# Two graph networks with residual layer norms on one core: the last layer norm's split rows turned by DMA instead of by TensorE

## The chip, the cores and the metric

The kernel runs on one core of a Trainium2 chip. The metric is the device time of one execution in microseconds (us), as the median of several runs. The profile is of one further execution, whose engines are named PE (TensorE; PEld are its weight loads), DVE (VectorE), ACT (ScalarE), POOL (GpSimd) and SP (SyncE, which here only issues DMAs).

## What is computed

The input `x` is 128 graphs x 128 nodes x 128 features. Two networks follow each other, each with a residual and a layer norm over the features:

```
x1  = layernorm(x  + gnn0(x,  adj))          # graph mix, two dense layers, batch norms
out = layernorm(x1 + gnn1(x1, adj))          # two graph layers, then the LSTM part

# LSTM part of gnn1, on h of shape (128 graphs, 128 nodes t, 128 features)
for p in 1, 2, 3, 4:
    nw   = 128 // p
    wins = h[:, :nw*p, :] as windows of p consecutive nodes
    last = last hidden state of LSTM_p over each window
    h[:, p-1::p, :] = last                   # the last node of each window is replaced
```

After the four periods, node `t` of `h` holds the state that period 4 wrote if `t % 4 == 3`; the other three of each four nodes hold what the periods 1 to 3 left there.

## The kernel before, in words

**The early part** (to about 350 us) computes `x1`, spills it to a scratch tensor in HBM, runs the two graph layers and, between them, the LSTM steps of period 1. The change does not touch its work. Two constants of it, `minus_c` and `u1_bias`, lie in SBUF and are last read there.

**The late part** is a list of LSTM steps, the units, written `p.tile.s` (period, tile of 4 windows x 128 graphs = 512 columns, step in the window). `LATE` gives the order of units 32 to 128 by hand. A first step (`s = 0`) has three gates of three 128x512 matmuls, 9 in all; a later step has four gates of six, 24 in all, since inputs and states are fp16 pairs of a high and a low half. For one unit, PE sums the gates into a ring of six PSUM banks (`lstm_unit`), ACT applies the gate functions (L894) and the tanh of the cell (L901), and DVE does `cell` (L1096, or L1099, L1101 and L1103), `hidden` (L1110), and splits the result into `hist`: `hidden_hi` (a cast, L1115) and `hidden_lo` (L1120). The last step of period 4 is `kept`: its result stays fp32 in `acts` and is not split.

**The last layer norm** is spread over the late part. Nodes are taken in 8 tiles of 16; a piece is one tile and one residue `r` of the node number modulo 4, so 4 nodes x 128 graphs. `hist` has the features on the partitions and the norm wants them on the free axis, so each piece is turned. For `r = 0, 1, 2` PE multiplies the high and the low half with an fp16 identity and sums them in PSUM: 8 matmuls (L798, L799, in `turn_h`). For `r = 3` PE transposes the four fp32 blocks of `acts` (L796). DVE adds the PSUM bank to the rows of `x1`, which a 1 MB load has brought into one of six SBUF buffers (`end_add`, L1175), then takes four row statistics (`end_row_stats`, L1182); after `r = 2` and after `r = 3` five small operations give the moments (`end_moments`, L1133 to L1140). POOL takes the power -1/2 (L534) and scales the rows (L544), and SP writes them out (L473). Once both parts of tile 0 (tile 1) are written, the buffer takes `x1` of tile 6 (7).

**The order** around the change is set by `ln_slots`, which places each piece at a unit number: PE turns it behind that unit, DVE adds it in the next unit between `cell` and `hidden`. SP follows the order of the moments. All engines wait only on semaphores in these fixed orders.

Of the kernel before, what the change touches and what calls it, by code (L numbers as in the profile page):

```python
# [8 lines left out]
ALU = mybir.AluOpType  # L9
# [142 lines left out]
def ln_slots():  # L152


    turns, adds, moments = {}, {}, {}
# [20 lines left out]
    for at, piece in sorted(places):  # L176
        put(turns, at, piece)
        put(adds, at + 1, piece)
        if piece[1] >= 2:
            put(moments, at + 1, (piece[0], 0 if piece[1] == 2 else 3))  # L180
    return turns, adds, moments


TURNS, ADDS, MOMENTS = ln_slots()


# [4 lines left out]
TURN_ORDER, ADD_ORDER, MOMENT_ORDER = (in_order(t) for t in (TURNS, ADDS, MOMENTS))  # L191
# [3 lines left out]
assert TURN_ORDER == ADD_ORDER  # L195
# [7 lines left out]
def resnorm_gnn_kernel(nc, x, adj, W1, b1, g1, be1, W2, b2, g2, be2,  # L203
# [15 lines left out]
    with ExitStack() as ctx:  # L219
# [24 lines left out]
        minus_c = sb("minus_c", [P, CB, P])  # L244
        u1_bias = sb("u1_bias", [P, CB, P])
# [99 lines left out]
        x1_loaded = [sem(f"x1_loaded{k}") for k in range(X1_RING)]  # L345
        h_turned, end_added, end_stats_done, end_step, end_var, end_rstd, end_scaled, tail_scaled = (
# [47 lines left out]
        def unit_cell(n):  # L394
            u = UNITS[n]
            if u.p == 1:
                return acts[:, n % 2, G, :]
            return cell_bufs[u.p, u.tile % CELLS[u.p]][:, 0:u.cols]

# [4 lines left out]
        def _(sp):  # L404
# [62 lines left out]
            for n, piece in enumerate(MOMENT_ORDER):  # L467
# [10 lines left out]
                if piece[1] == 3 and tile + X1_RING < TILES:  # L478
                    sp.wait_ge(out_written[tile % X1_RING], 32 * (tile // X1_RING + 1))
                    load_x1(tile + X1_RING)  # L480
            for k in range(X1_RING):
# [4 lines left out]
        def _(pool):  # L486
# [42 lines left out]
            for n, piece in enumerate(MOMENT_ORDER):  # L529
# [6 lines left out]
                if n >= N_POOLED:  # L536
                    continue
# [8 lines left out]
                last.then_inc(end_scaled, 1)  # L546

        @block.tensor
        def _(pe):
# [233 lines left out]
            def turn_h(tile, r):  # L783

                n = TURN_ORDER.index((tile, r))
                last = NUMBER[Unit(4, tile, 3)]
                if r == 3:
                    pe.wait_ge(hid_done, last + 1)
                else:
                    pe.wait_ge(lo_done, halves_through(max(NUMBER[v] for v in sources(Unit(4, tile, 0)))))  # L790
                wait(pe, end_added, n - 1)
                for m in range(CB):
                    t = tile * T_TILE + 4 * m + r
                    acc = ps[:, TURN + n % 2, m * P:(m + 1) * P]
                    if r == 3:
                        done = nc.tensor.transpose(acc, acts[:, last % 2, O, m * P:(m + 1) * P], ident[:])  # L796
                        continue
                    nc.tensor.matmul(acc, hist[:, 0, t, :], ident16[:], start=True, stop=False)  # L798
                    done = nc.tensor.matmul(acc, hist[:, 1, t, :], ident16[:], start=False, stop=True)  # L799
# [26 lines left out]
            for n in range(N_EARLY, len(UNITS)):  # L826
                lstm_unit(n)
                for tile, r in TURNS.get(n, ()):
                    turn_h(tile, r)
# [134 lines left out]
        def _(dve):  # L964
# [188 lines left out]
            def relu_h0(g, h):  # L1153
                dve.wait_ge(h0_summed, 2 * g + h + 1)
                nc.vector.tensor_tensor(h0T[:, h * CB:(h + 1) * CB, :].rearrange("p b n -> p (b n)"), ps[:, H0[h], :],  # L1155
                                        minus_c[:].rearrange("p b n -> p (b n)"), ALU.max).then_inc(h0_copied, 1)

            def bias_u1(g, h):
                dve.wait_ge(u1_summed, 2 * g + h + 1)
                nc.vector.tensor_tensor(u1[:, h * CB:(h + 1) * CB, :].rearrange("p b n -> p (b n)"), ps[:, U1[h], :],  # L1160
                                        u1_bias[:].rearrange("p b n -> p (b n)"), ALU.add).then_inc(u1_copied, 1)
# [8 lines left out]
            def end_add(tile, r):  # L1170
                n = ADD_ORDER.index((tile, r))
                rows = x1_tile[tile % X1_RING].rearrange("p (m r) d -> p r m d", r=4)[:, r, :, :]
# [4 lines left out]

            def end_row_stats(tile, r):
                rows = x1_tile[tile % X1_RING].rearrange("p (m r) d -> p r m d", r=4)[:, r, :, :]
                dve.wait_ge(end_added, ADD_ORDER.index((tile, r)) + 1)  # L1180
# [3 lines left out]
            def end_moments(piece):  # L1184
                n = MOMENT_ORDER.index(piece)
                tile, rows = piece[0], moment_rows(piece)
                dve.wait_ge(end_stats_done, CB * (ADD_ORDER.index((tile, rows.stop - 1)) + 1))
# [118 lines left out]
```

## Time and profile before

| | us |
|---|---|
| median of 3 runs (lowest, highest) | 757.35 (756.95, 757.46) |
| the profiled execution, its own time | 757.01 |
| its span (first to last instruction) | 755.2 |
| PE busy | 737.3 |
| DVE busy | 657.6 |
| ACT busy | 538.8 |
| POOL busy | 316.5 |

The time of the profiled execution is 1.8 us more than its span, and 0.34 us below the median. A row of the timeline gives start, duration, engine, line, operation, and in brackets the idle time just before it. Matmuls are pipelined: a row says 0.38 us for a 128x512 matmul, while the next one starts 0.22 us after it. DVE operations overlap a little too; what one costs is read from start to start. A row of a stretch gives its bounds and length, then the busy time (and instructions) of PE, PEld, DVE, ACT and POOL, the granted TensorE clock as a share of full speed, the DMA share and GB/s.

### The profile page before, as it was taken

The page shows a single profiled execution, that of the slowest core. Times are in us where ns is not written, and L with a number is a line of the kernel's source. Part 1 is how long each engine was busy: PE and PEld are TensorE (multiplying, and loading weights), DVE is VectorE, ACT ScalarE, POOL GpSimd, SP SyncE. Part 2 cuts the span into 40 slices and gives each one's busy share as a digit, 9 for nine tenths or more (in the row PEclk, how much of TensorE's full clock was granted, in tenths as well). Part 3 has the DMA queues.
Part 4 walks back from the last instruction along what each step waited for, and adds up shares of the span by engine and source line. Part 5 has one row for each costly group of instructions (what it writes and reads, how often), then busy time and mean ns, then how long its engine had stood idle before and what let it go on. Part 6 is the DMA issues. An engine that isn't in the chain of part 4 may idle for free.

```text
span 755.2 us, 11504 instructions
## 1 busy us (share of the span) xinstructions
PE 737.3 (98%) x4016; PEld 426.6 (56%) x4016; DVE 657.6 (87%) x1391; ACT 538.8 (71%) x872; POOL 316.5 (42%) x287
## 2 busy tenths in 40 slices
PE   8999999999999999998999999999999999999994
PEld 6777644677777777673444444444444444554542
DVE  6888787888998989858998799889999898899987
ACT  4877898467777686659887686786676767666662
POOL 1000000159788887800000001600981946239986
PEclk9999999999999999999999999999999999999997
DMA  5642400024424334114300000100000121021012
GB/s 158 189 140 87 112 1 1 1 56 112 112 57 113 83 86 111 30 29 193 141 1 2 0 1 1 43 1 0 28 35 24 38 75 43 1 70 57 15 56 85
DMA packets 64606, 45.08 MB, mean 60 GB/s; under 512 B 1658, under 2 KB 63524, under 8 KB 63524
## 3 DMA queue, kind: packets, MB, share of 16 engines
q1 hardware_dynamic: 64548, 44.33, 19.2%
q8 instruction: 33, 0.54, 0.3%
q14 instruction: 25, 0.20, 0.1%
HBM read 27.55 MB, written 16.78 MB: 59 GB/s over the span
## 4 chain that ended last, share of the span: by engine, by line
PE 53%; DVE 15%; ACT 6%; issue 2%; POOL 1%; DMA 1%; POOLq 0%; DVEq 0%; SPq 0%
PE ps L660 10%; PE ps L661 10%; PE ps L669 10%; PE ps L674 7%; PE ps L665 7%; PE ps L666 7%; ACT work L894 4%; DVE ln_stats L1146 2%; DVE ring L1127 2%; DVE store L1166 2%; DVE ring L1155 2%; DVE work L1110 1%; ACT work L901 1%; DVE work L1096 1%; DVE ring L1160 1%
## 5 line engine op out<-in xcount | busy, mean ns | idle before, releaser
L894 ACT ACTIVATE work<-ps,gate_bias 128x512 f32<-128x512 f32 x449 | 282.6, 680 | 91.1 <-PE ps L674 57.9
L660 PE MATMUL ps<-store,wih 128*128 128x512 f16 (+1 forms) x443 | 166.7, 376 | 2.3 <-ACT work L894 2.3
L661 PE MATMUL ps<-store,wih 128*128 128x512 f16 (+1 forms) x443 | 166.7, 376 | 0.0
L669 PE MATMUL ps<-store,wih 128*128 128x512 f16 (+1 forms) x443 | 156.0, 376 | 0.0
L534 POOL TENSOR_TENSOR end_mv<-end_mv,minus_half 128x12 f32<-128x12 f32 (+1 forms) x16 | 31.0, 1940 | 256.0 <-DVE end_mv L1140 256.0
L525 POOL TENSOR_SCALAR ring<-ring,ln_mv 128x128 f32<-128x128 f32 x112 | 113.3, 1024 | 2.8 <-POOL ln_mv L513 2.7
L1110 DVE TENSOR_TENSOR work<-work 128x512 f32<-128x512 f32 (+1 forms) x129 | 88.2, 684 | 22.5 <-ACT work L901 22.5
L901 ACT ACTIVATE work<-store 128x512 f32<-128x512 f32 x97 | 60.5, 623 | 52.7 <-DVE store L1103 36.2
L665 PE MATMUL ps<-store,whh 128*128 128x512 f16 (+1 forms) x248 | 93.2, 376 | 0.0
L666 PE MATMUL ps<-store,whh 128*128 128x512 f16 (+1 forms) x248 | 93.1, 376 | 0.0
L674 PE MATMUL ps<-store,whh 128*128 128x512 f16 (+1 forms) x248 | 93.0, 376 | 0.0
L544 POOL TENSOR_SCALAR ring<-ring,end_mv 128x128 f32<-128x128 f32 x72 | 85.7, 1202 | 1.4 <-POOL end_mv L534 1.4
L1120 DVE TENSOR_TENSOR store<-work,store 128x512 f16<-128x512 f32 (+1 forms) x121 | 81.9, 676 | 1.4 <-ACT store L926 1.4
L660 PEld LDWEIGHTS ps<-store,wih 128*128 128x128 f16 x443 | 43.4, 98 | 53.1 <-issue 8.2
L669 PEld LDWEIGHTS ps<-store,wih 128*128 128x128 f16 x443 | 43.3, 98 | 50.9 <-DVE store L1120 0.3
L661 PEld LDWEIGHTS ps<-store,wih 128*128 128x128 f16 x443 | 43.3, 98 | 48.3 <-issue 5.0
L505 POOL TENSOR_SCALAR bn_rstd<-mean_var 128x1 f32<-128x1 f32 x3 | 0.6, 193 | 134.0 <-DVE mean_var L1062 76.2
L544 POOL TENSOR_SCALAR store<-store,end_mv 128x128 f32<-128x128 f32 x48 | 54.9, 1156 | 1.1 <-POOL end_mv L534 1.1
L845 ACT ACTIVATE store<-ps,vec 128x512 f32<-128x512 f32 x64 | 40.5, 684 | 13.5 <-PE ps L589 13.4
L1099 DVE TENSOR_TENSOR work<-work 128x512 f32<-128x512 f32 (+1 forms) x62 | 42.3, 682 | 8.5 <-ACT work L894 7.5
L1031 DVE BATCH_NORM_STATS2 st<-store 128x6 f32<-128x512 f32 x64 | 41.2, 685 | 8.7 <-ACT store L845 8.6
L1101 DVE TENSOR_TENSOR store<-work,store 128x512 f32<-128x512 f32 (+1 forms) x62 | 42.1, 680 | 7.5 <-ACT work L894 7.4
(135 smaller groups left out, 1285.8 us busy)
## 6 DMA issues: line engine op xcount, KB each, us to landing
ring<-in_x_dram SPq DMA_DIRECT2D x32, 256.0 KB, 2.9
ring<-in_x_dram SPq DMA_DIRECT2D x16, 512.0 KB, 5.3
x_scratch<-ring SPq DMA_DIRECT2D x16, 512.0 KB, 3.5
ring<-x_scratch SPq DMA_DIRECT2D x5, 1024.0 KB, 4.9
out_dram<-ring SPq DMA_DIRECT2D x5, 768.0 KB, 3.5
store<-x_scratch SPq DMA_DIRECT2D x3, 1024.0 KB, 14.0
out_dram<-store SPq DMA_DIRECT2D x3, 768.0 KB, 3.9
out_dram<-ring SPq DMA_DIRECT2D x5, 256.0 KB, 2.3
```

Source lines behind the costliest of these rows:

```text
L525: last = nc.gpsimd.tensor_scalar(row, row, mv[:, 1, b:b + 1], mv[:, 4, b:b + 1], ALU.subtract, ALU.mult)
L544: last = nc.gpsimd.tensor_scalar(row, row, mv[:, 1, k:k + 1], mv[:, 4, k:k + 1], ALU.subtract, ALU.mult)
L660: nc.tensor.matmul(acc(j), w_hi, x_hi, start=True, stop=False)
L661: nc.tensor.matmul(acc(j), w_lo, x_hi, start=False, stop=False)
L665: nc.tensor.matmul(acc(j), w_hi, h_hi, start=False, stop=False)
L666: nc.tensor.matmul(acc(j), w_lo, h_hi, start=False, stop=False)
L669: last = nc.tensor.matmul(acc(j), weights(wih, j)[0], x_lo, start=False, stop=u.first)
L674: nc.tensor.matmul(acc(j), weights(whh, j, 1)[0], h_lo, start=False, stop=True)\
L894: nc.scalar.activation(acts[:, n % 2, gate, 0:u.cols], ps[:, gate_bank(q), 0:u.cols], ACT.Tanh if gate == G else ACT.Sigmoid, bias=gate_bi ...
L901: nc.scalar.activation(tanh_c[:, n % 2, 0:UNITS[n].cols], unit_cell(n), ACT.Tanh)\
L1110: nc.vector.tensor_tensor(hid, hid, tanh_c[:, n % 2, 0:u.cols], ALU.mult).then_inc(hid_done, 1)
L1120: nc.vector.tensor_tensor(unit_output(u, 1), columns(acts[:, n % 2, O, :], u), unit_output(u, 0), ALU.subtract).then_inc(lo_done, 1)
```

## The change

- PE no longer turns the pieces with `r < 3`; `turn_h` keeps `r = 3` alone.
- SP turns them instead (`move_rows`). Per tile it issues 8 transposing DMAs from `hist` to a new buffer `h_rows`: for each half (high, low) and each group of 4 nodes, 128 x 384 fp16 values become 3 blocks of 128 x 128. That is 96 KB each and 768 KB a tile, 64 DMAs in all.
- `h_rows` holds one tile. It lies over `minus_c` and `u1_bias`, and the first DMA of a tile waits until DVE has added the whole tile before (`h_added`).
- DVE adds a piece in two steps, high rows and then low rows, both from SBUF (`add_halves`); the second waits for the first, and each waits for its half's DMAs (`h_moved`).
- `ln_slots` places the pieces anew: a tile is moved one unit after its last source has run, and its first piece is added at the earliest four units after that. So the pieces of a tile come earlier than before in some places, and in the order of tiles 0 to 7.
- On SP the moves and the output writes are interleaved by unit number, a write standing four units behind its moments (`OUT_DELAY`).

```diff
     for tile in range(P // T_TILE):
-        ready = max(NUMBER[v] for v in sources(Unit(4, tile, 0))) + 2
-        wanted.append((max(ready, NUMBER[Unit(4, tile, 0)]), tile))
+        written = max(NUMBER[v] for v in sources(Unit(4, tile, 0)))
+        put(moves, written + 1, tile)
+        wanted.append((written + 4, tile))
...
+            def move_rows(tile):
+                n = MOVE_ORDER.index(tile)
+                sp.wait_ge(lo_done, halves_through(max(NUMBER[v] for v in sources(Unit(4, tile, 0)))))
+                wait(sp, h_added, 6 * n)
+                for s in range(2):
+                    for m in range(CB):
+                        t = tile * T_TILE + 4 * m
+                        sp.dma_start(h_rows[:, s, 3 * m:3 * m + 3, :],
+                                     hist[:, s, t:t + 3, :].rearrange("p t b -> p (t b)"),
+                                     transpose=True).then_inc(h_moved[s], 16)
...
-                    t = tile * T_TILE + 4 * m + r
-                    acc = ps[:, TURN + n % 2, m * P:(m + 1) * P]
-                    if r == 3:
-                        done = nc.tensor.transpose(acc, acts[:, last % 2, O, m * P:(m + 1) * P], ident[:])
-                        continue
-                    nc.tensor.matmul(acc, hist[:, 0, t, :], ident16[:], start=True, stop=False)
-                    done = nc.tensor.matmul(acc, hist[:, 1, t, :], ident16[:], start=False, stop=True)
+                    done = nc.tensor.transpose(ps[:, TURN + n % 2, m * P:(m + 1) * P],
+                                               acts[:, last % 2, O, m * P:(m + 1) * P], ident[:])
...
+            def add_halves(tile, r):
+                n = MOVE_ORDER.index(tile)
+                rows = x1_tile[tile % X1_RING].rearrange("p (m r) d -> p r m d", r=4)[:, r, :, :]
+                dve.wait_ge(x1_loaded[tile % X1_RING], 16 * (tile // X1_RING + 1))
+                for s in range(2):
+                    dve.wait_ge(h_moved[s], 16 * CB * (n + 1))
+                    wait(dve, h_added, 6 * n + 2 * r + s)
+                    nc.vector.tensor_tensor(rows, h_rows[:, s, :, :].rearrange("p (m r) d -> p r m d", r=3)[:, r, :, :],
+                                            rows, ALU.add).then_inc(h_added, 1)
```

Which pieces stand in which unit, by `ln_slots` (unit numbers; `(tile, r)`):

| tile | added before, r = 0, 1, 2 | moved now | added now, r = 0, 1, 2 |
|---|---|---|---|
| 0 | 62, 63, 64 | 59 | 63, 64, 65 |
| 1 | 81, 82, 83 | 69 | 73, 74, 75 |
| 2 | 77, 78, 79 | 72 | 76, 77, 78 |
| 3 | 90, 91, 92 | 82 | 86, 87, 88 |
| 4 | 98, 99, 100 | 92 | 96, 98, 99 |
| 5 | 111, 112, 113 | 94 | 100, 101, 102 |
| 6 | 117, 118, 119 | 113 | 117, 118, 119 |
| 7 | 121, 122, 124 | 116 | 120, 121, 122 |

The order of DVE's instructions in units 74 to 77 (3.5.0, 3.7.0, 4.2.0, 3.5.1), before, from `hidden` of unit 74 on. L1110 is `hidden`, L1115 and L1120 the two halves, L1096 the `cell` of a first step.

```order
671 L1110 TENSOR_TENSOR work<-work 128x512
672 L1115 CAST store<-work 128x512
673 L1096 TENSOR_TENSOR store<-work 128x512
674 L1120 TENSOR_TENSOR store<-work,store 128x512
675 L1110 TENSOR_TENSOR work<-work 128x512
676 L1115 CAST store<-work 128x512
677 L1096 TENSOR_TENSOR store<-work 128x512
678 L1120 TENSOR_TENSOR store<-work,store 128x512
679 L1110 TENSOR_TENSOR work<-work 128x512
```

The same stretch now, where the lines of these operations are L1135, L1140, L1145 and L1121, with the piece (1, 2), its moments and the piece (2, 0):

```order
677 L1121 TENSOR_TENSOR store<-work 128x512
678 L1145 TENSOR_TENSOR store<-work,store 128x512
679 L1210 TENSOR_TENSOR ring<-turned,ring 128x4x128 x2
680 L1220 BN_STATS end_stats<-ring 128x6 x4
681 L1158 TENSOR_TENSOR end_mv<-end_stats 128x12
...
685 L1165 SCALAR_TENSOR_TENSOR end_mv<-end_mv 128x12
686 L1135 TENSOR_TENSOR work<-work 128x512
687 L1140 CAST store<-work 128x512
688 L1121 TENSOR_TENSOR store<-work 128x512
689 L1145 TENSOR_TENSOR store<-work,store 128x512
690 L1210 TENSOR_TENSOR ring<-turned,ring 128x4x128 x2
691 L1220 BN_STATS end_stats<-ring 128x6 x4
```

Each `x2` is the high and the low add of one piece. Between the last add of tile 1 (row 679) and the first of tile 2 (row 690) stand the statistics, the moments, `hidden`, the cast, `cell` and the low half.

On SP, where the rows before held output writes and two loads alone, this stands now from the first move on:

```order
60 L485 DMA_TRANSPOSE turned<-store 128x3x128 x16
61 L496 DMA out_dram<-ring 128x4x384
62 L485 DMA_TRANSPOSE turned<-store 128x3x128 x8
63 L496 DMA out_dram<-ring 128x4x384
64 L485 DMA_TRANSPOSE turned<-store 128x3x128 x8
65 L496 DMA out_dram<-ring 128x4x384
66 L485 DMA_TRANSPOSE turned<-store 128x3x128 x8
```

Eight transposing DMAs a tile; the moves of tiles 0 and 1 follow each other directly, and each later one stands behind the write of an earlier tile.

## Rows read from the trace of the kernel before

**Rows 1.** The page's first part: busy time and share of the span, whole run.

```profile
PE 737.3 (98%) x4016; PEld 426.6 (56%) x4016; DVE 657.6 (87%) x1391; ACT 538.8 (71%) x872; POOL 316.5 (42%) x287
```

**Rows 2.** Chain of waits, 352 to 745 us: shares by line; then start us, us, what.

```profile
by line: PE ps L660 18.4%; PE ps L661 18.3%; PE ps L669 18.3%; PE ps L674 13.1%; PE ps L665 13.1%; PE ps L666 13.1%; PE ps L799 1.4%; PE ps L798 1.4%; PE ps L796 0.7%; ACT work L894 0.4%; DVE store L1101 0.3%; issue 0.3%; DVE end_stats L118
...
352.02 0.70 ACT work L894
...
737.18 0.70 ACT work L894
```

**Rows 3.** Who waited for whom, 352 to 743 us: engine line, releaser, us, times, longest.

```profile
ACT work L894 <- PE ps L674: 57.3, 110, 1.1
...
PE ps L660 <- ACT work L894: 0.5, 1, 0.5
```

**Rows 4.** Busy time of the engines in four stretches of the late stage.

```profile
443.70:505.30 61.60, 61.60 (x304) 28.59 (x303) 55.70 (x102) 46.20 (x73) 16.72 (x13) 1.00 0.04 14
505.30:590.30 85.00, 85.00 (x449) 40.74 (x448) 79.58 (x167) 59.09 (x95) 43.12 (x31) 1.00 0.06 20
590.30:651.80 61.50, 61.50 (x325) 30.73 (x324) 53.10 (x107) 42.22 (x70) 33.70 (x27) 1.00 0.14 48
651.80:743.50 91.70, 91.70 (x500) 46.02 (x499) 84.73 (x210) 57.53 (x92) 71.93 (x60) 1.00 0.13 42
```

**Rows 5.** PE in order of time, the turn after unit 3.6.1: start us, us, engine, line.

```profile
564.10 0.22 PE L798 MATMUL ps<-ident,store 128*128 128x128 f16 x1
...
564.54 0.38 PE L660 MATMUL ps<-store,wih 128*128 128x512 f16 x1
```

**Rows 6.** The turn's matmuls by line, whole run: duration ns min/median/max.

```profile
L798 PE MATMUL ps<-ident,store x96: 219/219/219, 447.4 to 717.0; 128*128 128x128 f16 x96
```

**Rows 7.** DVE in order of time, hidden(n) of units 82 to 86.

```profile
540.73 0.67 DVE L1110 TENSOR_TENSOR work<-work 128x512 f32<-128x512 f32 x1
...
545.36 0.69 DVE L1110 TENSOR_TENSOR work<-work 128x512 f32<-128x512 f32 x1
...
547.87 0.69 DVE L1110 TENSOR_TENSOR work<-work 128x512 f32<-128x512 f32 x1 [0.17 <-ACT work L901]
...
551.93 0.69 DVE L1110 TENSOR_TENSOR work<-work 128x512 f32<-128x512 f32 x1 [0.17 <-ACT work L901]
...
556.00 0.69 DVE L1110 TENSOR_TENSOR work<-work 128x512 f32<-128x512 f32 x1 [0.16 <-ACT work L901]
```

**Rows 8.** DVE in order of time, one whole unit (3.8.1) with a piece.

```profile
602.03 0.69 DVE L1110 TENSOR_TENSOR work<-work 128x512 f32<-128x512 f32 x1
...
605.77 0.68 DVE L1175 TENSOR_TENSOR store<-ps,store 128x512 f32<-128x512 f32 x1
606.49 0.87 DVE L1182 BATCH_NORM_STATS2 end_stats<-store 128x6 f32<-128x128 f32 x4
607.28 0.67 DVE L1110 TENSOR_TENSOR work<-work 128x512 f32<-128x512 f32 x1
```

**Rows 9.** DVE in order of time, first and last hidden of the 70 units summed.

```profile
443.72 0.69 DVE L1110 TENSOR_TENSOR work<-work 128x512 f32<-128x512 f32 x1 [0.16 <-ACT work L901]
...
745.77 0.69 DVE L1110 TENSOR_TENSOR work<-work 128x512 f32<-128x512 f32 x1 [0.16 <-ACT work L901]
```

**Rows 10.** DMA: the queue (packets, MB, share); issues with us to landing; SP's issues.

```profile
q1 hardware_dynamic: 64548, 44.33, 19.2%
...
store<-x_scratch SPq DMA_DIRECT2D x3, 1024.0 KB, 14.0
...
out_dram<-ring SPq DMA_DIRECT2D x5, 256.0 KB, 2.3
...
348.57 1.28 SPq L458 DMA_DIRECT2D ring<-x_scratch  x3
```

**Rows 11.** Busy time and granted clock after the last gate (same columns as rows 4).

```profile
743.50:746.50 3.00, 0.56 (x5) 0.32 (x3) 2.80 (x6) 1.32 (x2) 2.82 (x4) 1.00 0.64 227
746.50:748.00 1.50, 0.66 (x4) 0.42 (x4) 1.43 (x10) 0.00 (x0) 1.25 (x3) 0.79 0.00 0
```

More of the change, by code:

```diff
@@ L152, in ln_slots @@
 def ln_slots():
-    turns, adds, moments = {}, {}, {}
+    moves, turns, stats, moments = {}, {}, {}, {}
     end = len(UNITS) - 1
@@ L176, in ln_slots @@
     for at, piece in sorted(places):
-        put(turns, at, piece)
-        put(adds, at + 1, piece)
+        if piece[1] == 3:
+            put(turns, at, piece)
+        put(stats, at + 1, piece)
         if piece[1] >= 2:
             put(moments, at + 1, (piece[0], 0 if piece[1] == 2 else 3))
-    return turns, adds, moments
-TURNS, ADDS, MOMENTS = ln_slots()
+    return moves, turns, stats, moments
+MOVES, TURNS, STATS, MOMENTS = ln_slots()
 def in_order(table):
     return [piece for n in sorted(table) for piece in table[n]]
-TURN_ORDER, ADD_ORDER, MOMENT_ORDER = (in_order(t) for t in (TURNS, ADDS, MOMENTS))
+MOVE_ORDER, TURN_ORDER, STAT_ORDER, MOMENT_ORDER = (in_order(t) for t in (MOVES, TURNS, STATS, MOMENTS))
+assert MOVE_ORDER == [tile for tile, r in STAT_ORDER if r == 0]
+OUT_DELAY = 4
 TAIL = MOMENTS[len(UNITS) - 1]
@@ L480, in _ @@
                     load_x1(tile + X1_RING)
+            for n in range(N_EARLY, len(UNITS) + OUT_DELAY):
+                for tile in MOVES.get(n, ()):
+                    move_rows(tile)
+                for piece in MOMENTS.get(n - OUT_DELAY, ()):
+                    write_rows(piece)
             for k in range(X1_RING):
@@ L527, in _, with scale_rows @@
                 last.then_inc(x1_ready, 1)
[L529 removed]
+            def scale_rows(piece):
+                n = MOMENT_ORDER.index(piece)
                 tile, rows = piece[0], moment_rows(piece)
@@ L546, in _ @@
                 last.then_inc(end_scaled, 1)
+            for n in range(N_EARLY, len(UNITS)):
+                for piece in MOMENTS.get(n, ()):
+                    scale_rows(piece)
         @block.tensor
@@ L827, in _ @@
                 lstm_unit(n)
-                for tile, r in TURNS.get(n, ()):
-                    turn_h(tile, r)
+                for tile, _ in TURNS.get(n, ()):
+                    turn_h(tile)
         @block.scalar
@@ L1246, in _ @@
                 if n < end:
-                    for tile, r in ADDS.get(n, ()):
-                        end_add(tile, r)
+                    for tile, r in STATS.get(n, ()):
+                        if r == 3:
+                            end_add(tile)
+                        else:
+                            add_halves(tile, r)
                         end_row_stats(tile, r)
@@ L1252, in _ @@
                 else:
-                    for tile, r in ADDS[end][:-1]:
-                        end_add(tile, r)
+                    for tile, _ in STATS[end][:-1]:
+                        end_add(tile)
                 hidden(n)
@@ L1257, in _ @@
                     hidden_hi(n)
-            for tile, r in ADDS[end]:
-                if (tile, r) == ADDS[end][-1]:
-                    end_add(tile, r)
+            for tile, r in STATS[end]:
+                if (tile, r) == STATS[end][-1]:
+                    end_add(tile)
                 end_row_stats(tile, r)
```

41 lines of the change are left out of this document (23 added, 18 removed).

## The prediction, made before the changed kernel was run

> **What bounds the kernel now.** Read the page's first part first: PE is busy for 737.3 us, 98% of the span, and DVE comes next with 87% [rows 1]. Then the chain of waits. From 352.02 us, where ACT ends the graph part, to 737.18 us every share above 0.7% is a line of PE, and the turns of the split rows, L798 and L799, hold 1.4% each [rows 2]. The waits say the same from the other side: ACT waited 57.3 us for sums of PE, and PE waited 0.5 us, once [rows 3]. So in the late stage PE is the bound, and the turns lie on the path.
>
> The stretches then show how near the next bound is. In the four of rows 4, 299.8 us together, PE has no gap, and DVE is busy for 55.70 + 79.58 + 53.10 + 84.73 = 273.1 us, which leaves 26.7 us idle [rows 4]. Not all of that is spare. A unit on a loaded DVE still shows a wait of 0.17 us before `hidden`, for the tanh of ACT [rows 7]. Over the 69 units of these stretches that is 11.7 us that no added work can take, since added work only moves it. **The real spare is about 15 us in 300.** An independent count agrees. Between `hidden` of unit 58 and of unit 128 lie 302.1 us [rows 9]; 21 first steps at 2.51 us and 49 later ones at 4.07 us [rows 7], with the pieces below, come to between 285 and 290 us.
>
> **What the change removes from PE.** Each of the 24 pieces costs PE eight small matmuls. One says 0.22 us [rows 6], but they overlap: from the start of the first to the start of the next unit's first matmul it is 564.54 - 564.10 = 0.44 us [rows 5]. 24 x 0.44 = 10.6 us leave PE. If PE stayed the bound, the profiled execution's 757.0 us would become 746.4 us.
>
> **What it adds to DVE.** Before, a piece is one add of 128x512 from PSUM and four statistics. The add starts at 605.77 and the statistics, which wait for it, at 606.49, so a dependent add costs 0.72 us; the statistics take 0.79 us more [rows 8]. Now there are two adds, the second dependent on the first. The operand from SBUF instead of PSUM should change nothing: `hidden`, with both operands in SBUF, takes 0.69 us against 0.68 us for the add [rows 7, 8]. The trace has no add that mixes fp16 and fp32 inputs alone, so between 0 and 0.72 us I take the upper end, as the same form and size. 24 x 0.72 = 17.3 us, on an engine with 15 us to spare: 2.3 us over the present end, and the 10.6 us of PE are gone with it. DVE becomes the bound.
>
> **The new places make it uneven.** A piece adds 5.25 - 4.07 = 1.2 us net to a later unit now [rows 7, 8], 1.9 us after the change. The moments add 0.7 us. Tiles 1 and 2 are now added back to back in units 73 to 78, of which 74, 75 and 76 are first steps, where PE needs 9 x 0.216 = 1.9 us and DVE 2.51 us without any piece. For units 73 to 79 PE needs 4 x 5.2 + 3 x 1.9 = 26.5 us, DVE 4 x 4.07 + 3 x 2.51 + 6 x 1.9 + 2 x 0.7 = 36.6 us. PE can run ahead of ACT by its six banks only, 1.5 later units or 7.8 us, so this burst alone stops PE for 2 us or more, depending on how far DVE lags when it begins. Units 96 to 102 carry seven pieces in the same way. Between the bursts, in units 66 to 72, 103 to 108 and 124 to 126, there is no split piece and DVE will catch up and idle, so part of the 15 us is out of reach. I take 4.5 us, three tenths of it, as an estimate (0 to 8).
>
> **The transposing DMAs.** SP has no work of its own, and their issue costs nobody else anything. What counts is the time L from the release of a tile's eight DMAs to the landing of the last. No row shows such a DMA. From below: three plain issues took 1.28 us, 0.43 us each, and an output of 256 KB landed 2.3 us after issue [rows 10]: 7 x 0.43 + 2.3 = 5.3 us. From above: three loads of 1 MB queued behind others took 14.0 us to land [rows 10], for a tile's 768 KB. In between, by packets: the queue moved 64548 in 19.2% of 16 x 755.2 us, 36 ns each on its engine [rows 10]. Cut into rows of 128 fp16 values, a tile has 3072 packets, 192 on each engine, 6.9 us; with 2.3 us to land L is 9.2 us. I take this, since it counts the pieces that a turned block must be written in. The Trainium skill ("Advanced Engine Details and Errata", X-Bar Transpose (TRN2)) says instead that transposing DMAs are as fast as plain ones, 350 to 400 GB/s; by that the data take some 2 us and the sum would come to rival 2, about 765 us. No row here shows which.
>
> Where is L hidden? For tiles 0, 1, 3, 4 and 6 the first add stands five units behind the last source: some 11 to 15 us by 5.2 and 1.9 us a unit. At 9.2 us they are covered. **Tiles 2, 5 and 7 are not.** The buffer holds one tile, so their DMAs start only with the last add of tile 1, 4 or 6, in units 75, 99 and 119, and the first add that needs them is in the very next unit. Between the two DVE has the statistics, the moments, `hidden`, the cast, `cell` and the low half. For a first step this is 545.36 - 540.73 - 0.72 = 3.9 us [rows 7], for the later step 5.25 - 0.72 + 0.7 = 5.2 us. The low rows are needed 0.7 us later. Cover in all: 3.9 + 5.2 + 3.9 + 3 x 0.7 = 15.1 us against 3 x 9.2 = 27.6 us. DVE stands still for 12.5 us, with `hidden`, hence the split halves that PE waits for, queued behind. As DVE is the bound by then, all of it counts. On SP the output writes queue behind these waiting moves; POOL's scaling is finished late anyway and the end does not move.
>
> **Sum**, against the profiled execution: 757.0 + 2.3 + 4.5 + 12.5 = 776.3 us. That execution lies 0.34 us under the median of the runs, within their spread, so I predict 776.
>
> **Rivals.**
> 1. *Faster: DVE takes it.* If the second add costs less than (15 - 4.5) / 24 = 0.44 us and L stays under some 5 us, DVE still fits below the old end, and PE's saving shows, down to 746.4 us if all of it does. For it: PE is the only bound today. Against it: every two-input operation of this size on DVE has 0.67 to 0.69 us [rows 7, 8], and even L's lower bound is 5.3 us. Chance 0.15.
> 2. *Slower, but only by DVE's work.* L is near 5.3 us: 757.0 + 2.3 + 4.5 + (15.9 - 15.1) = 764.6 us. Chance 0.17, and 0.03 that pieces and stage gains cancel to no change.
> 3. *Much slower: the DMAs run one behind the other.* If each transposing DMA takes its own 2.3 us to land before the next moves, L is 8 x 2.3 = 18.4 us. Then the three bare hand-overs cost 55.2 - 15.1 = 40.1 us and the five others about 5 x (18.4 - 14.5) = 19.5 us: 757.0 + 6.8 + 59.6 = 823 us. It decides from L above some 14 us. For it: the trace has no transposing DMA that would exclude it. Chance 0.20. The Trainium skill ("VectorE: DVE Perf Modes", The three transpose paths) gives 1309 ns for one 128x128 block by DMA; 24 blocks in a row would be 31 us, further on this side than any row.
>
> A smaller cost sits in all of them: after PE had been nearly idle for 3 us, the granted clock of the next stretch was 0.79 [rows 11]. Stops of PE at the three hand-overs could cost about 1 us each this way; it is in the range, not in the sum.
>
> **How the numbers follow.** The forecast (L between 6 and 14 us, 767 to 794 us) has 0.45. The range of 752 to 825 us takes in rivals 2 and 3 and the milder part of rival 1, and leaves out the full gain and an L above 18 us. Faster by over 0.2% (what a measurement of this kernel can tell from no change) 0.15, within 0.2% 0.03, slower 0.82.
>
> **What would show it.** In the profile after: no L798 or L799 rows; DVE at over 90% of the span; PE with idle time in the late stage whose releaser is DVE's cast or low half, none of which it has now; DVE's high-rows add waiting for a DMA at three places, first after unit 75, by some 4 us each; landing of the transposing DMAs of 9 us a tile; the dependent adds 0.72 us apart. It would be wrong if PE still showed no gap, if the adds took clearly under 0.7 us, or if tiles 0, 1, 3, 4 and 6 waited too.

## The result, and the profile after

The changed kernel takes **798.54 us** (median of 4 runs, 797.52 to 798.67), the kernel before 757.40 us beside it (4 runs, 756.95 to 757.57). The ratio is 1.054, with a 95% interval of 1.0527 to 1.0553: slower by 41 us, where 18.6 us were forecast. 798.5 us lies inside the predicted range, and above the 767 to 794 us that the forecast's own case allowed. Two runs in a slow state are left out of every number below: one of experiment 5 (1093.89 us, at a granted clock of 0.654) and one of the kernel before (780.88 us, at 0.946).

The first part of the page of the kernel after, which answers to [rows 1], its row of PE in tenths, the queue that moves the tiles (packets, MB, share of the 16 DMA engines), and the chain by engine; the last row is the chain of the kernel before:

```profile
span 796.7 us, 11215 instructions
PE 737.4 (93%) x3824; PEld 415.8 (52%) x3824; DVE 674.2 (85%) x1415; ACT 535.3 (67%) x872; POOL 305.7 (38%) x287
PE   8999999999999999989999999858999958999394
q1 hardware_dynamic: 91172, 50.63, 22.3%
DVE 35%; PE 23%; ACT 10%; issue 5%; SPq 4%; DMA 2%; POOL 1%; DVEq 0%; POOLq 0%
PE 53%; DVE 15%; ACT 6%; issue 2%; POOL 1%; DMA 1%; POOLq 0%; DVEq 0%; SPq 0%
```

DVE was busy for 674.2 - 657.6 = 16.6 us more, the 24 added adds at 0.69 us each. PE, with 192 matmuls fewer, now has gaps (the 5, 5 and 3 in its row of tenths). DVE leads the chain now, and SP's queue and the DMAs are in it; before, PE led it, and in the late part it was nearly PE alone [rows 2].

The same four stretches as [rows 4], by time from the span's start (they hold fewer units now):

```profile
443.70:505.30 61.60, 59.67 (x276) 26.49 (x274) 56.37 (x104) 44.76 (x72) 16.76 (x13) 1.00 0.17 39
505.30:590.30 85.00, 71.55 (x319) 31.07 (x317) 73.60 (x156) 47.34 (x78) 37.10 (x30) 0.94 0.15 38
590.30:651.80 61.50, 55.04 (x250) 24.44 (x248) 53.01 (x110) 34.59 (x57) 32.89 (x28) 0.94 0.27 73
651.80:743.50 91.70, 79.78 (x391) 38.21 (x388) 72.10 (x162) 53.42 (x90) 44.48 (x40) 0.96 0.17 45
```

PE is idle for 13.5 of the 85.0 us of the second stretch, and DVE for 11.4, against 5.4 us before: DVE is not busier than it was, it stands still. The waits from 350 us on say for what (engine, line, releaser, us, times, longest; L926 is ACT's tanh of the cell, L1210 the new adds, L694 the first matmul of a gate, L823 the turn of `r = 3`):

```profile
ACT work L926 <- DVE store L1128: 94.1, 62, 10.6
PE ps L694 <- ACT work L919: 24.8, 10, 8.2
PE ps L823 <- DVE work L1135: 15.2, 2, 13.0
DVE ring L1210 <- DMA turned<-store: 8.7, 2, 4.4
DVE ring L1210 <- issue: 6.4, 2, 3.2
DVE store L1210 <- DMA turned<-store: 4.4, 1, 4.4
DVE store L1210 <- issue: 1.2, 1, 1.2
```

The last four are the waits of the first adds of tiles 2, 5 and 7 and of no others, 7.6, 5.6 and 7.5 us: 8.7 + 6.4 + 4.4 + 1.2 = **20.7 us**. PE, which waited for ACT for 0.5 us before [rows 3], now waits for ACT and for `hidden` (once for 13.0 us, behind the wait of tile 7), and those wait for DVE.

One hand-over in full. DVE in order of time (start, us, engine, line, operation, idle before) from the last add of tile 1 to the first of tile 2, in unit 76:

```profile
513.28 1.48 DVE L1210 TENSOR_TENSOR ring<-turned,ring 128x512 f32<-128x512 f16 x2
514.79 0.87 DVE L1220 BATCH_NORM_STATS2 end_stats<-ring 128x6 f32<-128x128 f32 x4
...
516.30 0.69 DVE L1135 TENSOR_TENSOR work<-work 128x512 f32<-128x512 f32 x1
...
517.96 0.68 DVE L1145 TENSOR_TENSOR store<-work,store 128x512 f16<-128x512 f32 x1
521.89 0.72 DVE L1210 TENSOR_TENSOR ring<-turned,ring 128x512 f32<-128x512 f16 x1 [3.25 <-issue]
526.99 0.69 DVE L1210 TENSOR_TENSOR ring<-turned,ring 128x512 f32<-128x512 f16 x1 [4.37 <-DMA turned<-store]
```

And the chain of waits over the same time (start, us, what), followed back from the end:

```profile
514.07 0.70 DVE ring L1210
514.83 1.19 SPq L485
516.06 1.26 SPq L485
517.36 1.26 SPq L485
518.66 1.26 SPq L485
519.96 1.26 SPq L485
521.25 1.98 SPq L485
523.27 1.26 SPq L485
524.58 2.39 DMA turned<-store
526.99 0.70 DVE ring L1210
```

The last add of tile 1 frees the buffer at 514.8. SP then needs about 1.26 us for **each issue** (each SPq row is one; the sixth took 1.98 us). The eighth starts at 524.58, and 2.4 us after this start its data are there: L = 526.99 - 514.83 = 12.2 us. For tiles 5 and 7 L was 11.4 and 12.1 us (the first issue at 629.04 and 730.08, the low add at 640.47 and 742.19). The four stretches of 10 us around the first hand-over, PE alone (busy, granted clock, DMA share, GB/s):

```profile
505.00:515.00 10.00, 6.97 (x32) 1.00 0.00 0
515.00:525.00 10.00, 9.91 (x46) 1.00 0.35 71
525.00:535.00 10.00, 1.85 (x5) 0.61 0.27 89
535.00:545.00 10.00, 8.84 (x36) 0.88 0.00 1
```

DVE stops at 518.6 us. PE works on with its six banks until 524.9 us, 6.3 us longer, where 7.8 us of run ahead were forecast, and then has nothing for 8.2 us. With the stop the mean granted clock of the stretch falls to 0.61, between its levels of 1.2 and 2.4 GHz. The transposing DMAs by themselves, whole run:

```profile
L485 SPq DMA_TRANSPOSE turned<-store x64: 1182/1257/2306, 446.6 to 739.8; - x64
DMA to landing us min/median/max: 2.3/2.4/4.1
```

The queue took (22.3% x 796.7 - 19.2% x 755.2) x 16 = 523 us of packet time for 91172 - 64548 = 26624 packets more than before [rows 10]. Put down to the 64 DMAs alone, as an estimate, that is 20 ns a packet and 523 / 64 / 16 = 0.5 us a DMA on each engine, against 1.26 us for its issue: the DMA engines were not the limit.

### The profile page after: what moved, and what is told of

Read it like the earlier page. It is cut to its first block, busy times and chain, and to the rows that moved or that the text cites. A ratio compares the mean times of both kernels' runs of the same rounds, so it can differ in the third digit from the quotient of the medians.

```text
span 796.7 us, 11215 instructions
## 1 busy us (share of the span) xinstructions
PE 737.4 (93%) x3824; PEld 415.8 (52%) x3824; DVE 674.2 (85%) x1415; ACT 535.3 (67%) x872; POOL 305.7 (38%) x287
## 3 DMA queue, kind: packets, MB, share of 16 engines
q1 hardware_dynamic: 91172, 50.63, 22.3%
## 4 chain that ended last, share of the span: by engine, by line
DVE 35%; PE 23%; ACT 10%; issue 5%; SPq 4%; DMA 2%; POOL 1%; DVEq 0%; POOLq 0%
ACT work L919 6%; DVE work L1135 4%; PE ps L694 4%; PE ps L695 4%; PE ps L703 4%; SPq L485 3%; ACT work L926 3%; PE ps L708 3%; PE ps L699 3%; PE ps L700 3%; DVE store L1126 3%; DVE store L1145 3%; DVE work L1124 2%; DVE ln_stats L1171 2%; DVE end_stats L1220 2%
## 5 line engine op out<-in xcount | busy, mean ns | idle before, releaser
L919 ACT ACTIVATE work<-ps,gate_bias 128x512 f32<-128x512 f32 x449 | 279.1, 680 | 72.4 <-PE ps L708 39.2
L694 PE MATMUL ps<-store,wih 128*128 128x512 f16 (+1 forms) x443 | 168.8, 381 | 26.2 <-ACT work L919 26.1
L695 PE MATMUL ps<-store,wih 128*128 128x512 f16 (+1 forms) x443 | 168.7, 381 | 0.0
L703 PE MATMUL ps<-store,wih 128*128 128x512 f16 (+1 forms) x443 | 157.3, 379 | 0.0
L926 ACT ACTIVATE work<-store 128x512 f32<-128x512 f32 x97 | 60.5, 623 | 115.7 <-DVE store L1128 94.1
L1135 DVE TENSOR_TENSOR work<-work 128x512 f32<-128x512 f32 (+1 forms) x129 | 89.0, 690 | 22.0 <-ACT work L926 22.0
L699 PE MATMUL ps<-store,whh 128*128 128x512 f16 (+1 forms) x248 | 95.0, 383 | 2.2 <-DVE store L1140 2.2
L708 PE MATMUL ps<-store,whh 128*128 128x512 f16 (+1 forms) x248 | 94.1, 380 | 1.6 <-DVE store L1145 1.6
L700 PE MATMUL ps<-store,whh 128*128 128x512 f16 (+1 forms) x248 | 94.9, 383 | 0.0
L694 PEld LDWEIGHTS ps<-store,wih 128*128 128x128 f16 x443 | 43.6, 98 | 85.2 <-ACT work L919 24.4
L1145 DVE TENSOR_TENSOR store<-work,store 128x512 f16<-128x512 f32 (+1 forms) x121 | 81.9, 677 | 1.4 <-ACT store L951 1.4
L574 POOL TENSOR_SCALAR ring<-ring,end_mv 128x128 f32<-128x128 f32 x72 | 78.2, 1098 | 1.4 <-POOL end_mv L564 1.4
L574 POOL TENSOR_SCALAR store<-store,end_mv 128x128 f32<-128x128 f32 x48 | 52.0, 1095 | 1.1 <-POOL end_mv L564 1.1
L1124 DVE TENSOR_TENSOR work<-work 128x512 f32<-128x512 f32 (+1 forms) x62 | 42.4, 684 | 11.7 <-ACT work L919 10.3
L870 ACT ACTIVATE store<-ps,vec 128x512 f32<-128x512 f32 x64 | 40.5, 683 | 13.5 <-PE ps L623 13.5
L1056 DVE BATCH_NORM_STATS2 st<-store 128x6 f32<-128x512 f32 x64 | 41.1, 685 | 8.7 <-ACT store L870 8.6
```

The lines of the kernel that those rows point to most:

```text
L574: last = nc.gpsimd.tensor_scalar(row, row, mv[:, 1, k:k + 1], mv[:, 4, k:k + 1], ALU.subtract, ALU.mult)
L694: nc.tensor.matmul(acc(j), w_hi, x_hi, start=True, stop=False)
L695: nc.tensor.matmul(acc(j), w_lo, x_hi, start=False, stop=False)
L699: nc.tensor.matmul(acc(j), w_hi, h_hi, start=False, stop=False)
L700: nc.tensor.matmul(acc(j), w_lo, h_hi, start=False, stop=False)
L703: last = nc.tensor.matmul(acc(j), weights(wih, j)[0], x_lo, start=False, stop=u.first)
```

## The experiments

The lines in the diffs are those of the kernel named. Theories have letters in the expectations; the text between names them by what they say. The kernel before ran beside each group and took between 757.1 and 757.6 us.

**1. The change without its DMAs** (`hist` is added unturned, at the new places):

```diff
-                for s in range(2):
-                    for m in range(CB):
-                        sp.dma_start(h_rows[:, s, 3 * m:3 * m + 3, :], ..., transpose=True)
...
-                                            h_rows[:, s, :, :]...[:, r, :, :]
+                                            hist[:, s, t:t + 13:4, :]
```

> The changed kernel without its 64 transposing DMAs; DVE adds rows of hist as they lie, so nothing is turned and the output is not the reference's. Theory A (the DMAs cost more than their three waits on DVE: each also leaves PE stopped, at a lower clock, and DVE idle while PE catches up): the time falls by far more than the 20.8 us that DVE waits for them, to about 764 us, as the forecast's sum without the hand-overs. Theory B (the DMAs cost their waits alone, and the rest is DVE's added work, none of which finds spare time): 798.5 - 20.8 = 778 us.

**775.89 us**, ratio 1.0246 (1.023 to 1.0262), near theory B. Taking the DMAs out gives back 22.6 of the 41.1 us, and 18.5 us stay with no transposing DMA in the kernel at all. Of the 22.6 us, 20.7 are the waits. Some 1.5 us more are the low add: in the 21 pieces that don't wait for a DMA it starts 0.79 us after the high one in the kernel after, and 0.72 us here, where it has one semaphore less to wait for.

**2. PE's part alone**: before, with `turn_h` returning at once for `r < 3`; DVE adds what lies in PSUM.

> The kernel before without the 192 matmuls that turn the split rows; DVE adds what lies in PSUM, so nothing is turned. PE's part of the change alone. If PE is the bound everywhere in the late stage: 757.4 - 10.6 = 747 us. If DVE is already the bound in bursts: 749 to 753 us.

**751.47 us**, 0.9927 (0.9911 to 0.9942). PE has 10.6 us less to do and the kernel gains 5.7, as expected for a DVE that is the bound already.

**3. DVE's part alone**: before, with a second, dependent add.

```diff
+                if r < 3:
+                    dve.wait_ge(end_added, n + 1)
+                    t = tile * T_TILE + r
+                    nc.vector.tensor_tensor(rows, hist[:, 1, t:t + 13:4, :], rows, ALU.add)
```

> The kernel before with a second, dependent add for each of the 24 split pieces, at the old places, PE still turning them (the second operand is the low half of hist unturned, so the output is not the reference's). DVE's part alone. Theory A (most of the 15 us spare can be used): 757.4 + 17.3 - 10.5 = 764 us. Theory B (spare is not where the pieces are): up to 757.4 + 17.3 = 775 us.

**769.62 us**, 1.0163 (1.0145 to 1.0181). Of 17.3 us of work 12.5 show, at the old places and with no DMA in it: between the two theories.

**4. Three units of room between tiles**: the change with one rule more in `ln_slots`.

```diff
+        at = max(at, free + GAP * (free > 0))
```

> The changed kernel with three units between the last piece of a tile and the first of the next, so that DVE waits for no DMA (tile 2 from unit 79, tile 5 from 103, tile 7 from 124). Theory A (a wait drags PE's stop, clock and idle behind it): near no_dma, about 764 to 768 us. Theory B (waits alone): about 778 us. A third possibility is that SP's slow issue shifts the waits elsewhere: over 785 us.

**776.72 us**, 1.0261 (1.0245 to 1.0277). All 64 DMAs run, and no add has a wait for them. The time is that of experiment 1 within 0.8 us, but this is chance, since the rule also changes the places and the end. The late stage, from `hidden` of unit 58 to that of unit 128, took 315.2 us here and 320.0 us in experiment 1. The end after it took 15.4 us in place of 9.5, because the last tile's moments now come so late that DVE's last scaling waits for POOL:

```profile
DVE ring L1243 <- POOL end_mv L568: 6.0, 1, 6.0
```

The 315.2 us are those of experiment 5 below (315.9), which has no transposing DMA and the old places. So 64 of them with room to land cost the late stage nothing that shows, and the room costs 6 us at the end.

**5 to 7. Places and adds apart.** Experiment 5 is experiment 1 at the old places; 6 is the kernel before with the new places (`ready = written + 4`, turns by PE); 7 is experiment 1 with the high rows' add alone (`for s in range(1)`).

> The changed kernel without its DMAs (rows of hist added unturned, as in no_dma) and with the split pieces back at the places of the kernel before. PE's and DVE's parts together, at the old places. Theory C (the two parts simply add up, and the rest of no_dma's 18.6 us comes from the new places): 757.3 - 5.8 + 12.4 = 764 us. Theory D (once PE no longer turns, DVE's second add is paid in full, wherever it stands): about 775 us, as no_dma.

> The kernel before, with the split pieces at the places of the changed kernel; PE turns them and DVE adds once. The places alone. Theory C: the bursts of six pieces on first steps and of seven in a row already overrun DVE with one add, 757.3 + 12 = 769 us. Theory D: the places cost nothing by themselves, 757 to 760 us.

> no_dma with one add a piece instead of two (the high rows alone), at the new places, PE turning nothing. Theory C: the pe_only time plus what the places cost, 751.5 + 12 = 763 us. Theory D: near pe_only, 752 to 755 us, so that the second add is worth 20 us or more there.

| | PE's turns | adds a piece | places | us | ratio, 95% interval |
|---|---|---|---|---|---|
| 5 | none | 2 | old | 771.00 | 1.0179 (1.0157 to 1.0201) |
| 6 | all | 1 | new | 760.64 | 1.0045 (1.003 to 1.006) |
| 7 | none | 1 | new | 758.37 | 1.0011 (1.0002 to 1.0021) |

Experiment 5 is the surprise: with PE's turns gone, the two adds cost 771.0 - 757.3 = 13.7 us where 2.3 us were forecast, before any new place; it lies between its two theories. The new places add 775.9 - 771.0 = 4.9 us to it. What they cost depends on the rest: 3.3 us with PE's turns and one add (experiment 6, 0.6 us above what theory D allowed), and 758.4 - 751.5 = 6.9 us without turns and with one add (experiment 7 against 2, between its theories).

**8 and 9. No add at all.** The next two kernels ask whether DVE held the time up already with one add. `end_add` returns for `r < 3` in both; 8 also leaves out PE's turns.

```diff
+                if r < 3:
+                    return
                 dve.wait_ge(h_turned, n + 1)
```

> The kernel before without PE's 192 matmuls for the split rows and without DVE's 24 adds of them (these parts of the result are left out). PE then has 10.6 us less and DVE 17.3 us less to do than before. Theory A, in pe_only DVE is already the bound of the late part: without the adds PE is the bound again and its whole saving shows, 757.3 - 10.6 = 747 us. Theory B, the 4.8 us that pe_only did not give lie outside of DVE's load (ends, hand-overs to ACT): as pe_only, 751.5 us.

> The kernel before without DVE's 24 adds of the split rows, PE still turning them (the sums are left out of the result). Theory A, PE alone is the bound before and DVE's adds lie beside it: 757.3 us, no change within 0.2%. Theory B, DVE holds PE up here and there already before: faster, by at most the 17.3 us of the adds, and something like 2 to 4 us.

8 took **746.27 us** (0.9856, 0.984 to 0.9872), 9 took **757.62 us** (1.0006, 0.9997 to 1.0015). Both times theory A. With the old places, the time by adds of a piece is now:

| us | no add | one add | two adds |
|---|---|---|---|
| PE turns | 757.6 | 757.4 | 769.6 |
| PE doesn't | 746.3 | 751.5 | 771.0 |

With PE turning, the first add is free: PE is the bound. Without, PE's own end is 746.3 us, as forecast (746.4), and the first add costs 5.2 us already: DVE sets the time from there on, and the second add costs all its 17.3 us and 2.2 more. The next two rows are sums and means of busy time over four stretches of the late stage, both without PE's turns: 292 us of experiment 2 (one add), then 287 us of experiment 8 (no add):

```profile
sum 292.00, PE 288.66 PEld 133.77 DVE 268.71 ACT 199.41 POOL 162.64; mean PE 72.17 PEld 33.44 DVE 67.18 ACT 49.85 POOL 40.66
```

```profile
sum 287.00, PE 287.00 PEld 134.34 DVE 255.28 ACT 204.01 POOL 162.25; mean PE 71.75 PEld 33.58 DVE 63.82 ACT 51.00 POOL 40.56
```

In the first DVE is idle for 23.3 us all the same, 8% of the stretch, and PE for 3.3 us, which it isn't in the second. DVE's waits there are for ACT (the tanh before `hidden`, the gates before `cell`), 16.4 us together; the other 6.9 us are gaps under 0.15 us, which this view leaves out:

```profile
DVE work L1113 <- ACT work L904: 9.3, 39, 0.8
DVE work L1102 <- ACT work L897: 4.9, 7, 1.1
DVE store L1104 <- ACT work L897: 2.2, 6, 0.5
```

**DVE's idle time, kernel by kernel**, from `hidden` of unit 58 to `hidden` of unit 128:

| kernel | stretch, us | DVE busy | DVE idle |
|---|---|---|---|
| before | 302.1 | 275.2 | 26.9 |
| 8: no turns, no add | 291.4 | 259.5 | 31.8 |
| 2: no turns, one add | 297.6 | 274.2 | 23.4 |
| 3: turns, two adds | 314.6 | 290.7 | 23.9 |
| 5: no turns, two adds | 315.9 | 291.3 | 24.6 |
| 4: three units of room | 315.2 | 291.6 | 23.6 |
| 1: new places, no DMAs | 320.0 | 292.5 | 27.5 |
| after | 343.2 | 291.9 | 51.3 (20.7 for DMAs) |

At the old places DVE was idle for 23 to 25 us whether it had 274 or 291 us of work. So of the 26.9 us before, 2.3 to 3.5 us could take work.

**10. The moves cut into blocks**: 24 DMAs of 128x128 a tile, 192 in all, in place of 8 of 128x384, with the same bytes.

```diff
-                    for m in range(CB):
...
-                        sp.dma_start(h_rows[:, s, 3 * m:3 * m + 3, :], ...)
+                    for k in range(3 * CB):
+                        sp.dma_start(h_rows[:, s, k, :], ...)
```

> The changed kernel with each transposing DMA of 128x384 cut into three of 128x128 (24 a tile, 192 in all), to see what SP's 1.26 us for each is paid for. If it is paid per instruction: 24 x 1.26 + 2.4 = 32.6 us from release to landing, every tile waits, some 798.5 + 3 x 20 + 5 x 18 = 950 us. If it is paid per block: SP issues each in some 0.42 us and the time stays at 798 us. In between, some fixed part and some part per block, which the row of the issue gives.

**943.8 us** in one run, near the 950 us of a price by instruction. Its transposing DMAs:

```profile
L484 SPq DMA_TRANSPOSE turned<-store x192: 1094/1233/2232, 446.4 to 885.0; - x192
```

A third of the bytes costs SP 1.23 us, as good as the same. Between these two sizes the price is one of the instruction, not of what it moves. DVE stands still before its high and low adds for 122.7 us by a DMA's landing and 44.1 us more that the same wait shows under "issue" (13.1 and 7.6 us in the kernel after).

**11. POOL adds tiles 0 to 5** (both halves of a whole tile in two operations of 128x1536; tiles 6 and 7 are turned by PE as before).

> An attempt at a better version: for tiles 0 to 5 the transposing DMAs stay, but POOL makes the high and low adds of a whole tile (two operations of 128x1536) and DVE only takes the statistics; tiles 6 and 7 are turned by PE and added by DVE as before. PE is freed of 18 x 0.44 = 7.9 us and DVE of 18 x 0.72 = 13 us, so with PE the bound 749 to 750 us. If POOL's adds slow DVE (both read SBUF) by over a tenth, or take over 8 us each and come late: 757 us or more.

**772.23 us**, 1.0199 (1.0183 to 1.0215), a miss by 22 us. POOL and then DVE, in order of time, around the first two of POOL's twelve adds:

```profile
452.61 3.18 POOL L578 TENSOR_TENSOR ring<-turned,ring 128x1536 f32<-128x1536 f16 x1 [131.58 <-DMA turned<-store]
457.72 3.52 POOL L578 TENSOR_TENSOR ring<-turned,ring 128x1536 f32<-128x1536 f16 x1 [1.93 <-DMA turned<-store]
452.38 0.43 DVE L1154 CAST store<-work 128x512 f16<-128x512 f32 x1
452.88 3.45 DVE L1138 TENSOR_TENSOR work<-work 128x512 f32<-128x512 f32 x1
456.26 0.68 DVE L1140 TENSOR_TENSOR store<-work,store 128x512 f32<-128x512 f32 x1
458.43 3.36 DVE L1149 TENSOR_TENSOR work<-work 128x512 f32<-128x512 f32 x1 [0.16 <-ACT work L940]
461.83 0.43 DVE L1154 CAST store<-work 128x512 f16<-128x512 f32 x1
```

A DVE operation that takes 0.69 us elsewhere takes 3.45 and 3.36 us here, and ends half a microsecond after POOL's add. Each of the twelve adds holds one DVE operation like this, for 3.2 to 3.6 us, until 0.3 to 0.55 us after its own end. Over the whole run DVE was busy for 677.4 us. It had 18 adds of 0.68 us fewer than before, so 657.6 - 12.2 = 645.4 us were due: twelve adds on POOL held it for 32 us, more than the 25.9 us that 36 adds of its own would take. That this is the whole of the 22 us is argued, not shown by a run. The Trainium skill ("GPSIMD Engine Reference", Specifications) says that POOL shares SBUF interfaces with VectorE and names DVE instructions with two SBUF inputs, or in a 2-port perf mode, as cases of contention. The trace agrees for the two held operations shown and for nine more of the twelve, which have two inputs from SBUF. The twelfth is a cast with one input (at 498.40 us, 3.23 us in place of 0.43); no run here shows its mode.

**12. Places by hand**, the change with its pieces in units where DVE had idle time (first adds of tiles 0 to 7 in units 66, 73, 82, 90, 96, 106, 117, 122).

> The changed kernel with its 24 split pieces put by hand into units where DVE stood idle in no_dma (later steps behind kept steps, and stretches with no piece): tile 0 in 66, 69, 71; 1 in 73, 78, 79; 2 in 82, 85, 86; 3 in 90, 91, 93; 4 in 96, 99, 100; 5 in 106 to 108; 6 in 117 to 119; 7 in 122, 124, 125. Only tile 7 should still wait for its DMAs, 1 to 2 us. If DVE's idle time was out of reach only because of where the pieces stood: pe_only plus 17.3 us less some 9 us that the idle units take, 760 to 764 us. If idle time moves with the pieces (DVE's work is simply paid): 769 to 773 us, as no_dma_old.

**780.11 us**, 1.0296 (1.0279 to 1.0313), a miss by 7 us of even the slower case. In the same stretch as in the table DVE was idle for 29.5 us of 321.5. It still waited for 4.5 us for its DMAs, and without these 25.0 us stay, as in experiment 5 (24.6): the idle time is no store to fill, it moves to other units. Against experiment 5 the stretch is 5.6 us longer, 4.5 of it these waits, and the end 2.6 us longer, since DVE's last scaling waits 3.0 us for POOL.

**13 and 14. High halves only**, one add a piece. These leave the low fp16 half of the split rows out of the last residual, so they compute less than the kernel before: 13 by PE (one matmul in place of two), 14 by DMA (32 in place of 64, two buffers of a tile, the old places but for tile 0, one unit later).

> The kernel before, turning the high halves alone: 96 of the 192 small matmuls are left out, and with them the low halves of the split rows in the last residual (a rounding of those rows to fp16). PE is freed of half of 10.6 us. With the measured worth of pe_only (5.8 of 10.6 us): 754 to 755 us. If the first half is worth its full price and only the second meets DVE: 752 us.

> The changed kernel with the high halves alone: 4 transposing DMAs a tile into one of two buffers, one add a piece, the pieces at the places of the kernel before (the low halves of the split rows are left out of the last residual, as in high_pe). No tile should wait: 4 x 1.26 + 2.4 = 7.4 us from release to landing. DVE has the work that it had before, and PE 10.6 us less: as pe_only, 751.5 us. If transposing DMAs disturb the other engines: 754 us or more.

**753.22 us** (0.9946, 0.9931 to 0.996), between its two cases, and **751.35 us** (0.9921, 0.9906 to 0.9936), as expected. The second is the time of experiment 2, which has no DMAs for it: 32 transposing DMAs, with room to land, cost nothing that shows, and no wait for one is in its trace. It is the fastest kernel here that still turns all rows, at the price of these rows' precision. No version was found that keeps both halves and beats the kernel before.

## Why the prediction was wrong in size

The direction held, and so did the outline: DVE becomes the bound, and three hand-overs wait. Two terms of the sum were too small, one by its size and one because its reasoning failed. Against 757.4 us, with the measured steps in the prediction's order:

| term | forecast | measured |
|---|---|---|
| DVE's second add, PE's turns gone | +2.3 | +13.7 (experiment 5) |
| the new places | +4.5 | +4.9 (experiment 1 against 5) |
| hand-overs | +12.5 | +22.6 (after against 1); 20.7 of waits |
| sum | +19.3 | +41.2 |

**The step that failed: "The real spare is about 15 us in 300."** It took the 26.7 us of idle time in [rows 4] and counted as out of reach only the waits before `hidden`, 11.7 us. The table of idle times shows what was out of reach: 23.4 us once DVE sets the time with one add (experiment 2), 24.6 us with two (experiment 5). The spare was 26.9 - 23.4 = 3.5 us, and 17.3 - 3.5 = 13.8 us should show; experiment 5 shows 13.7, and experiment 3, with PE's turns, 12.5. DVE's waits in the same stretches of the kernel before, which the prediction did not look up, name a part of what was missed:

```profile
DVE work L1110 <- ACT work L901: 9.3, 39, 0.8
DVE store L1101 <- ACT work L894: 5.6, 15, 0.5
DVE work L1099 <- ACT work L894: 5.1, 8, 1.2
```

Beside the tanh (9.3 us) stand 10.7 us of waits for the gates of ACT at `cell`. In experiment 2, where DVE sets the time, 4.9 + 2.2 = 7.1 us of them are still there, so only a third gave way. The remaining 6.9 us are gaps under 0.15 us, as many in experiment 2. That they belong to the hand-overs between ACT and DVE within a unit is a reading of these rows; no run takes them away.

The second count in the prediction, 285 to 290 us from `hidden` of unit 58 to that of unit 128, does not come out of its own prices. The stretch holds 31 pieces and 14 sets of moments: 21 x 2.51 + 49 x 4.07 + 31 x 1.2 + 14 x 0.7 = 299.1 us. Seven of the later steps are `kept` and lack the cast and the low half (0.43 + 0.68 us), which leaves 291.3 us. So the count already left 3 to 11 us of spare and did not confirm 15. It also has no waits at `cell`, since its steps come from back-to-back units without them; in experiment 2 that way takes 741.27 - 443.68 = 297.6 us. Two adds cost 771.0 - 751.5 = 19.5 us against one, 2.2 more than their work. Of this the traces show 24.6 - 23.4 = 1.2 us of idle time; the other 1 us is open.

**Hand-overs: the term was mis-sized by L.** The cover was right: the forecast had 3.9 us before the first add of tile 2, and DVE's rows of the hand-over above have 518.64 - 514.76 = 3.9 us. L was 12.2, 11.4 and 12.1 us, not 9.2: 35.7 - 15.1 = 20.6 us, against 20.7 us of waits. The prediction looked for L in the data (3072 packets at 36 ns) and took the issue at 0.43 us from a plain DMA. It is the other way round: by the estimate above the packets took 20 ns each and 0.5 us a DMA, and the issue took 1.26 us, three times that of [rows 10]. Rival 3 had the right shape, one DMA behind the other, with the wrong price (2.3 us each). The Trainium skill's sentence that transposing DMAs are as fast as plain ones ("Advanced Engine Details and Errata", X-Bar Transpose (TRN2)) holds here for the landing, 2.4 us against 2.3 us of a plain output, and not for the issue. Its 350 to 400 GB/s are not reached either: 96 KB in 0.5 us is some 190 GB/s, by the same estimate. Its 1309 ns for one 128x128 block ("VectorE: DVE Perf Modes", The three transpose paths) is near the 1233 ns that an issue took in experiment 10, though the page doesn't say what its time covers. 1257 ns were also enough for three blocks, so a tile cost 10 us of issues and not 31 us.

**The places** came out near the estimate, 4.9 against 4.5 us, and this is in part luck: 4.5 was three tenths of a spare of 15 us that isn't there, and the same places cost 3.3 and 6.9 us in experiments 6 and 7. That back-to-back pieces are what costs fits experiment 4: with three units between the tiles its late stage is as short as at the old places. The steps came out: a first step with a piece takes 511.02 - 506.47 = 4.55 us and a later one with piece and moments 541.14 - 534.53 = 6.61 us, against 2.51 + 1.9 and 4.07 + 1.9 + 0.7.

**PE's saving** was right, 10.6 us forecast and 11.1 us measured (757.4 - 746.3), and of no use: with two adds it makes 771.0 against 769.6 us, no gain. **The price of an add** from SBUF with mixed fp16 and fp32 inputs was right as a duration, 0.69 us. From the high add to the low one it was 0.79 us in the kernel after (two adds in a row of 1.48 us above) and 0.72 us in experiments 1 and 5. **The end** did not move, as said: 9.5 us from the last `hidden` on, before and after.

**What would show it**: DVE's wait for DMAs at exactly three places and no wait for tiles 0, 1, 3, 4 and 6 came true. The waits were 7.6, 5.6 and 7.5 us a place, not some 4, and L 11.4 to 12.2 us, not 9. PE's stops came mostly through ACT (24.8 us) and `hidden` (15.2 us), and only 3.8 us of them behind the cast and the low half. The adds were 0.79 us apart, not 0.72. DVE was at 85% of the span, not over 90%, since its idle share stays.

**The clock** cost little. The late stage had 0.94 in the mean, yet it was 343.2 - 320.0 = 23.2 us longer than that of experiment 1 (0.98), with 20.7 us of waits and 1.5 us of later low adds in it. That leaves 1.0 us for the clock and PE's restarts.

## What to carry to other kernels

Idle time on the second-busiest engine is not spare by itself. Take the bound away in a kernel of its own and see where the next engine ends, before work is moved onto it. Here that end lay 6 us under the old one, where idle time said 15, and 8% idle remained on the engine that set the time. Where a single buffer is handed over, its refill time, less what the waiting engine has to do meanwhile, counts in full. Count the refill's instructions first and its bytes second, and leave room or a second buffer before the first use, but see what the room does to the end: in experiment 4 it gave back the waits and cost 6 us there. When two kernels take the same time, compare them by stage before calling their causes the same.

## What the runs showed of the hardware

- A transposing DMA costs SP's queue 1.26 us at 128x384 fp16 and 1.23 us at 128x128, against 0.43 us for a plain one [rows 10]. It lands 2.4 us after the start of its issue, and its packets took about 20 ns each, by the estimate above. 32 of them with room to land changed nothing (experiment 14).
- A two-input POOL operation on SBUF (128x1536, 3.3 us) holds one DVE operation until it has ended: eleven of two inputs, 0.69 us otherwise, and one cast (experiment 11).
- A DVE add behind one that it depends on starts 0.72 us after it in experiment 1 and 0.79 us after it in the kernel after, where one more semaphore is waited for between the two; that the semaphore is the cause is not shown.
- In a stop of PE the granted clock of a 10 us stretch fell to 0.61, and the next stretch had 0.88, after one of 1.00 in which PE was busy for 9.91 us.
